# Gated linear attention: projections two tiles ahead, states as 64-row matmuls, f32r parts

## The reference

```python
q1 = (x @ Wq).reshape(B, L, H, DK) * scale          # H = 8 heads of DK = 64
k1 = (x @ Wk).reshape(B, L, H, DK)
v  = (x @ Wv).reshape(B, L, H, DV)
q2 = (x @ Wqa @ Wqb).reshape(B, L, H, DK) * scale   # low rank, 64
k2 = softmax((x @ Wka @ Wkb).reshape(B, L, H, DK))
gk1 = log_sigmoid(x @ Wg1a @ Wg1b + bg1) / 16       # low rank, 16
gk2 = log_sigmoid(x @ Wg2a @ Wg2b + bg2) / 16
e = softmax(x @ We); mask = one_hot(top_1(e)); rw = e * mask      # 4 experts
o = gla(q1, k1, v, gk1) + sum over experts of gla(q2 * rw, k2 * rw, v, gk2 * mask)
g = x @ Wga @ Wgb
o = rms_norm(o) * norm_w * (g * sigmoid(g))
return o @ Wo
```

## Time and profile before

| | us |
|---|---|
| median of 3 runs (lowest, highest) | 5345.69 (5344.24, 5350.46) |
| span of the profiled execution | 5273.1 |
| outside the span (median less span) | 72.6 |
| low_rank | 4213.0 to 4320.5 |
| linear_attention | 4320.5 to 5273.1 |
| TensorE busy, whole span | 4750.9 (90%) |
| VectorE busy, whole span | 4145.9 (79%) |
| ScalarE busy, whole span | 3061.5 (58%) |
| GpSimd busy, whole span | 1117.5 (21%) |

### The profile page before, as it was taken

The page is one execution under the profiler, slowest core; times in us unless marked ns, Lnnn a source line. Parts: engine busy times, 40 slices in busy tenths (PEclk is TensorE's granted clock), DMA queues, the critical chain, the costliest instruction groups (busy, mean ns, idle before and its releaser), DMA issues. The chain is left out here.

```text
span 5273.1 us, 101047 instructions
## 1 busy us (share of the span) xinstructions
PE 4750.9 (90%) x39176; PEld 2433.6 (46%) x39176; DVE 4145.9 (79%) x5059; ACT 3061.5 (58%) x5260; POOL 1117.5 (21%) x1152
## 2 busy tenths in 40 slices
PE   5579999999999999999999988558999969999998
PEld 3223333333333333333333356435666646666666
DVE  4489999999999999999999233377765447877877
ACT  1138888888888888888888712112222225555554
POOL 0000011202112021121211220254420004344443
PEclk8669999999999999999999999879999979999999
DMA  5434422322222222222221127632210030110100
...
DMA packets 236953, 421.64 MB, mean 80 GB/s; under 512 B 36745, under 2 KB 141210, under 8 KB 236432
## 3 DMA queue, kind: packets, MB, share of 16 engines
...
## 5 line engine op out<-in xcount | busy, mean ns | idle before, releaser
L956 DVE TENSOR_REDUCE attn_mpart<-attn_ps_max 128x2 f32<-128x1024 f32 x2048 | 2474.7, 1223 | 94.8 <-PE attn_ps_max L1007 85.1
L821 ACT ACTIVATE attn_probs<-attn_ps_exp 128x512 f32<-128x512 f32 x4096 | 2230.6, 595 | 411.0 <-PE attn_ps_exp L1023 331.3
L1007 PE MATMUL attn_ps_max<-attn_keys,attn_quer 54*128 54x512 f32 x4096 | 1474.0, 461 | 104.5 <-DVE attn_mpart L956 62.4
L1023 PE MATMUL attn_ps_exp<-attn_quer,attn_keys 54*128 54x512 f32 x4096 | 1513.3, 448 | 21.8 <-DMA attn_quer<-m_rows 20.7
L1038 PE MATMUL attn_ps_out<-attn_probs,attn_vals 128*32 128x256 f32 x16384 | 1312.1, 392 | 9.8 <-ACT route_o L826 9.2
L1023 PEld LDWEIGHTS attn_ps_exp<-attn_quer,attn_keys 54*128 54x128 f32 x4096 | 620.0, 185 | 860.1 <-ACT attn_probs L821 769.3
L1038 PEld LDWEIGHTS attn_ps_out<-attn_probs,attn_vals 128*32 128x32 f32 x16384 | 323.6, 108 | 750.8 <-issue 416.4
L1007 PEld LDWEIGHTS attn_ps_max<-attn_keys,attn_quer 54*128 54x128 f32 x4096 | 589.5, 189 | 169.7 <-DVE attn_mpart L956 106.0
L577 POOL DMA_INDIRECT x_rows<-route_pay,route_now x256 | 252.3, 985 | 431.7 <-DMA x_rows<-route_pay,route_now 359.5
L1576 POOL DMA_INDIRECT ra_rows<-y_rows,slots x256 | 255.5, 998 | 316.2 <-DVE ra_total L1743 244.5
L1707 ACT ACTIVATE ra_row<-ra_psS 128x512 f32<-128x512 f32 x112 | 66.9, 597 | 369.9 <-PE ra_psS L1628 369.9
...
## 6 DMA issues: line engine op xcount, KB each, us to landing
attn_keys<-k_laid SPq DMA_DIRECT2D x256, 304.0 KB
attn_vals<-v_aug SPq DMA_DIRECT2D x128, 512.0 KB, 16.1
attn_keys<-k_laid SPq DMA_DIRECT2D x256, 128.0 KB
...
```

Of the source, the lines that this page charges most:

```text
L821: act.activation(probs[k % 2][:, j, :], ps_exp[bank_of(g, n)][:, :], ACT.Exp).then_inc(exp_done, 1)
L956: dve.tensor_reduce(mpart[i][:, kb, TC * pair + tile::TC * NPR], ps_max[buffer][:, :, :], AX, ALU.max).then_inc(unit_read, 1)
L1007: mm = pe.matmul(ps_max[buffer][:, h, :], quer[at % NG][half(h), pair, tile * P:(tile + 1) * P], keys[at % 2][half(h), pair, kb * CH:(kb + ...
L1023: pe.matmul(ps_exp[bank_of(g, n)][:, :], keys[g % 2][half(h), pair, k * P:(k + 1) * P], quer[g][half(h), pair, :], start=True, stop=True). ...
```

## The change

What it does, by parts:

- **Four tiles in an iteration**: far, nxt, cur, prv. Z1, Z2 and ZG are made for far, between and behind the two halves of inter(cur); the rest of nxt's items in the next iteration. run has one more iteration to fill.
- **Order of TensorE**: turn_feats, scores 0, K2 Q2, decay_sums, keys_values, V, scores 1, turn_o, intra, G1 G2, project_o, K1 Q1, inter of two pairs, Z1 Z2 of far, inter of the others, ZG of far. ScalarE: decays(cur) ahead of abs and exp of nxt. VectorE: states are aged with the next tile's mean square; decay_states and log_sigmoid stand ahead of the second mask.
- **f32r parts**: every projection is made of f32r matmuls. Operands are split into a high part (a copy) and the rest (a subtraction): V, K1, Q1 are 6 matmuls each instead of 2 (high x high, high x low, low x high, for 2 blocks of rows), G1, G2 two each, ZG, K2, Q2 two each (both parts stacked in 128 rows), Z1, Z2 one each (three parts in 48 rows). In all 30 f32r matmuls of 512 columns per tile. The splits are new work: weights in low_rank (ScalarE 128x3072, 128x4096 and 128x128, GpSimd the rests), low in low_rank (ScalarE and GpSimd, 128x1024 per chunk), hT in linear_attention (hch on ScalarE, hcl on GpSimd, 128x256 per tile) and the log sigmoids (lsh on ScalarE, lsl on VectorE, 128x1024 per tile).
- **States without zero blocks**: s_mid is 128x1280 for a tile instead of 128x2560; inter is 40 matmuls of 64 rows and 64 columns, odd heads in one PSUM bank and even ones in another. decay_states, the addition and the ageing are one operation each over 128 partitions, and the addition is cut in two (dense, experts). pdec shares a bank of psO, so decay_sums waits until the former sums have been read (o_read), and intra waits for dec.
- **Space and DMAs**: xres's space holds ke and the states, so rope_attention stores xres to DRAM (x_mid, 8 stores of 512 KB) and linear_attention loads a tile of it for the output, which is one addition now (gb is multiplied into wo). low_rank stores 12 pieces of low per chunk instead of one. Linear_attention's weights load in low_rank. A tile has 7 loads instead of 4, and that of x_mid.

The diff, cut to its core:

```diff
+        def store_rows(sp, c):
+            sp.wait_ge(step, added(c * TC + TC - 1))
+            tiles = slice(c * TC, (c + 1) * TC)
+            sp.dma_start(x_mid[:, tiles, :], xres[:, tiles, :]).then_inc(x_stored, 16)
...
-                        hold(sp, low_copied, 2 * (c + 1), sp_passed)
-                        sp.dma_start(low_d[:, :, bass.ds(c * CH, CH)], low[i][:, :, :]).then_inc(low_stored[i], 16)
+                        hold(sp, low_parts, c + 1, sp_passed)
+                        n = bass.ds(c * CH, CH)
+                        high, rest = lowh[i], lowl[i]
+                        for g, r in ((0, LOW_G1[1]), (1, LOW_G2[1])):
+                            for x, part in enumerate((high, rest, high)):
+                                sp.dma_start(lz_d[g, x * GLR:(x + 1) * GLR, n],
+                                             part[r:r + GLR, 1, :].bitcast(F32)).then_inc(low_stored[i], 16)
+                        for x, (b, r) in enumerate((LOW_GATE, LOW_K, LOW_Q)):
...
+                act.wait_ge(g_loaded, 112)
+                act.wait_ge(tri_step, 5)
+                act.activation(gw.qkv[0][:, :, :, :], qkv[:, :, :, :], ACT.Copy).then_inc(w_high, 1)
+                act.activation(gw.up[:, :, :], up[:, :, :], ACT.Copy).then_inc(w_high, 1)
...
+        def run(eng, first, iteration, epilogue):
+
+            first((0, 0, 0))
+            iteration((1, 0, 1), (0, 0, 0), None, None)
+            iteration((2, 1, 0), (1, 0, 1), (0, 0, 0), None)
+            iteration((3, 1, 1), (2, 1, 0), (1, 0, 1), (0, 0, 0))
...
+                def iteration(far, nxt, cur, prv):
+                    if prv is not None:
+                        square(prv)
+                    if cur is not None:
+                        copy_feats(cur)
                     if nxt is not None:
-                        log_sigmoids(nxt, cur)
-                    else:
+                        copy_gate(nxt)
+                    if cur is not None:
                         decays(cur)
                     if nxt is not None:
+                        log_sigmoids(nxt)
```

```diff
-                def iteration(nxt, cur, prv):
+                def iteration(far, nxt, cur, prv):
                     if prv is not None:
                         mean_square(prv)
-                    if nxt is not None:
-                        add_bias(nxt)
-                        center(nxt)
-                    mask_scores(cur, 0)
-                    if prv is not None:
+                        age(prv)
                         scale_o(prv)
                         gated(prv)
-                    mask_scores(cur, 1)
+                    if cur is not None:
+                        mask_scores(cur, 0)
+                    if nxt is not None:
+                        center(nxt)
+                    if cur is not None:
+                        decay_states(cur)
                     if nxt is not None:
                         log_sigmoid(nxt)
-                    decay_states(cur)
-                    add_to_states(cur)
+                    if cur is not None:
+                        mask_scores(cur, 1)
+                        add_dense(cur)
+                    if nxt is not None:
+                        split_ls(nxt)
+                    if cur is not None:
+                        add_experts(cur)
```

```diff
-                        mm = pe.matmul(ps, (cen[:, :], m2c[i][:, 1, :])[x], ls[i][:, x, :], start=True, stop=True)
+                        pe.wait_ge(ls_low, m + 1)
+                        for part in (lsh, lsl):
+                            mm = pe.matmul(ps, (cen[:, :], m2g[i][:, :])[x], part[:, x, :], start=(part is lsh),
+                                           stop=(part is lsl))
...
+                                mm = pe.matmul(ps, h_part[:, k, :], w_part[:, x, k, :], start=(k == 0 and w_part is wqkv[0]
+                                               and h_part is hch), stop=(k == KD - 1 and h_part is hcl))
+                    elif item in (Z1, Z2):
+                        mm = pe.matmul(ps, lcz[i][:, :], wup[:, (UP_Z1, UP_Z2)[item - Z1], :], start=True, stop=True)
...
-                        (b, r), rows = {Z1: (LOW_G1, GLR), Z2: (LOW_G2, GLR), ZG: (LOW_GATE, LORA), K2: (LOW_K, LORA),
-                                        Q2: (LOW_Q, LORA)}[item]
-                        mm = pe.matmul(ps, lc[i][r:r + rows, b, :], wup[r:r + rows, b, :], start=True, stop=True)
+                        x, blocks = {ZG: (0, (UP_GATE, UP_GATE_LOW)), K2: (1, (UP_K, UP_K_LOW)),
+                                     Q2: (2, (UP_Q, UP_Q_LOW))}[item]
+                        for n, block_ in enumerate(blocks):
+                            mm = pe.matmul(ps, lcg[i][:, x, :], wup[:, block_, :], start=(n == 0), stop=(n == 1))
...
+                    pe.wait_ge(o_read, m)
...
+                    pe.wait_ge(dec_exped, m + 1)
+                    for odd in (1, 0):
+                        if odd == 0:
+                            pe.wait_ge(dense_read, m + 1)
...
+                def inter(tile, pairs):
                     m, _, i = tile
                     pe.wait_ge(state_set, m + 1)
                     pe.wait_ge(qe_ready, m + 1)
-                    for b in range(NPAIR):
-                        o = psO[:, 2 * b:2 * b + 2, :].rearrange("p h d -> p (h d)")
+                    for b in pairs:
                         for e in range(NS):
-                            queries = qeT[:, b, e - 1, :] if e else ftT[:, 1, b, :]
-                            mm = pe.matmul(o, queries, s_mid[:, b, e, :, :].rearrange("p h d -> p (h d)"),
-                                           start=False, stop=(b == NPAIR - 1 and e == NE), skip_group_check=True)
-                    mm.then_inc(intra_inter, 1)
-
-                def iteration(nxt, cur, prv):
+                            for odd in range(2):
+                                rows = slice(odd * DK, odd * DK + DK)
+                                queries = qeT[rows, b, e - 1, :] if e else ftT[rows, 1, b, :]
+                                mm = pe.matmul(heads_out[:, b, odd, :], queries, s_mid[rows, b, e, :], start=False,
+                                               stop=(b == NPAIR - 1 and e == NE), skip_group_check=True)
+                    if pairs[-1] == NPAIR - 1:
+                        mm.then_inc(intra_inter, 1)
...
+                def iteration(far, nxt, cur, prv):
                     ahead = lambda *items: [project(nxt, x) for x in items] if nxt is not None else None
-                    ahead(Z1, Z2)
-                    turn_feats(cur)
-                    ahead(ZG, K2)
-                    scores(cur, 0)
-                    decay_sums(cur)
-                    scores(cur, 1)
-                    ahead(Q2, V)
+                    if cur is not None:
+                        turn_feats(cur)
+                        scores(cur, 0)
+                    ahead(K2, Q2)
+                    if cur is not None:
+                        decay_sums(cur)
+                        keys_values(cur)
+                    ahead(V)
+                    if cur is not None:
+                        scores(cur, 1)
                     if prv is not None:
                         turn_o(prv, cur)
-                    keys_values(cur)
+                    if cur is not None:
+                        intra(cur)
+                    ahead(G1, G2)
                     if prv is not None:
                         project_o(prv, cur)
-                    ahead(G1, G2)
-                    intra(cur)
                     ahead(K1, Q1)
-                    inter(cur)
-
-                def prologue(tile):
-                    for x in range(NP):
+                    if cur is not None:
+                        inter(cur, (0, 1))
+                    if far is not None:
+                        project(far, Z1)
+                        project(far, Z2)
+                    if cur is not None:
+                        inter(cur, (2, 3))
+                    if far is not None:
+                        project(far, ZG)
+
+                def first(tile):
+                    for x in (Z1, Z2, ZG):
```

334 lines of the change are left out of this document (211 added, 123 removed).

## The result

| | median us (lowest to highest, runs) |
|---|---|
| before | 5344.97 (5335.64 to 5350.46, 4) |
| changed | 5499.26 (5458.79 to 5514.64, 4) |
| ratio | 1.0274, 95% interval 1.0226 to 1.0322 |

The changed kernel is slower by 154 us. The time lies 0.74 us inside the upper end of the range, which is luck: part of the 154 us isn't the change's, and the second comparison, which says 111, would have lain well inside. That later comparison of the same two kernels gave 5470.70 (5461.84 to 5497.61, 4 runs) against 5359.95, ratio 1.0229 (1.0180 to 1.0278).

A forecast was written before the change was run, and what follows sets the result against it. TensorE's own list bounds the kernel now; after the change a closed chain across engines would. Chain +37.5, clock dips +32 and edges +15 made +84.5 us on the median 5345.7: 5430, range 5310 to 5500.

The forecast's parts named there:

- The closed chain: linear_attention's loop: waits across TensorE, ScalarE and VectorE set a tile at 29.22 us against 27.97, +37.5 in 30.
- K1,Q1: Term of a tile's chain on TensorE: 12 f32r matmuls at 0.213 us each, 2.56 in all.
- The clock: linear_attention's tiles: 3 us idle brings dips in most, 1.5 us each, +32 net (bounds 0 and +84).
- The 64-row matmuls: Rival, inter: pairs pass in half the time, 4.56 to 2.28 us, total 5330 or 5294; chance 0.26.
- An f32r matmul at 0.33: Rival, projections: 24 f32r matmuls on the path cost 2.8 us more a tile, +84, total 5515; chance 0.14.
- a clock that holds: Rival, tile loop: the chain lengthens tiles but adds no dips, total 5398 (5380 to 5410); chance 0.20.
- The second chain: After inter: square, root, scale_o and gate could delay decay_sums; costed at nothing, with a microsecond to spare.
- x_mid's tail: End of rope_attention: the last 512 KB store of x_mid must land first, +3.7 us.
- Start of linear_attention: Weights no longer load there, so TensorE's first matmul comes at 7 us instead of 15.3: -8.
- SyncE's stores: low_rank: 13 stores issued per chunk instead of 2, 7.0 to 8.5 us a chunk, +5.5 (0 to +11).
- ScalarE's copies and GpSimd's subtractions: low_rank: weight copies ahead of the softmax's exp +6.9 us, subtractions beside the small softmax steps +3.
- the 72.6 us outside the span stay: Whole launch: median 5345.7 less profiled span 5273.1 was taken as fixed, so the +84.5 was added to the median.

The follow-up runs named there:

- y3: The changed kernel with the six matmuls of V issued three times over in each tile: 5353.44 us, ratio 1.0131 to the kernel before.
- x1: The kernel before with only x_mid's eight stores added in rope_attention, read by nobody: 5351.17 us against 5366.06, ratio 0.9989.

## Why the prediction was right, and where it was short

**The closed chain.** Right, term by term but one. From the tile above, measured against forecast: first feature turn to scores 3.19 (3.17); scores 1.09 (1.09); K2,Q2 1.13 (1.05); decay_sums to dec's end 1.36 (1.35); abs to the log sigmoid 5.83 (5.72); G1,G2 1.03 (1.05); from project_o to K1 2.19 (2.10); inter with Z1,Z2 5.41 (5.39); ZG 0.57 (0.63). Log sigmoid and masks to intra took 3.40 (3.03), with the turn of o already at the lower clock. The one term that was clearly too small is K1,Q1, 3.00 instead of 2.56: at full clock an f32r matmul of 512 columns follows the one before after 0.233 us, not after the 0.213 that I had worked out from the clock and not from a row, and the first of the twelve and the change of shape cost 0.1 each on top. At full clock the chain is 29.98 us (y3), forecast 29.22.

**The clock.** Right in kind: a dip in every tile, in the turn of o and intra, behind the wait. I took 1.5 us for each, and it is 31.62 - 29.98 = 1.64. That this came so near is luck: half of a full dip was a guess between bounds of 0 and 3.24. Of the signs, the tiles of 31.1 to 32.6 us lie above the 29 to 31 that I named, and low_rank's 22 above the 10 to 20. Over 30 tiles the loop is 948 us, forecast 922: 23 us of the difference is the chain's 0.76, 4 the clock.

**Rivals.** The 64-row matmuls don't pass in half the time: inter is two pieces of 2.37 and 2.38 us, each with a change of shape, for what took 4.56 before. The price of pairs was rightly read from the scores; that the loading of the weights sets it, as I wrote, no run here tests. An f32r matmul at 0.33 and a clock that holds are refuted too. The second chain, by way of scale_o, was never last: on VectorE the normalised output is done at 4917.8, and decay_sums starts at 4918.24. Its cover was 0.5 us and not the microsecond that I gave it; the ageing of the states now stands beside GpSimd's first small step and makes that 1.07 us longer (last section).

**The edges.** x_mid's tail 3.6 us (3.7). Start of linear_attention 6 us earlier (8): the first matmul comes at +9.3. SyncE has issued the seven loads 4.4 us into the stage, and the last one has landed only 4.9 us later; the 2.5 us that I put there had no row. Filling: the first inter comes 62.0 us into the stage (62.3 before), so the new stage costs what the start gains, 6 (4). low_rank +22.0 (15.4): the mis-sized term is SyncE's stores, +16.7 instead of +5.5. From the first store of hT to the last lie 69.1 us instead of 52.4: 9 of it is the last six chunks at 8.6 us, just above my upper bound of 8.5, and 7.7 is the gap behind the first chunk (result), which I had not thought of. Behind the last store the stage is 5.4 us longer, where I had 9.9 for ScalarE's copies and GpSimd's subtractions. One term was missing: in the last full iteration, which has no far and no nxt, nothing hides the waits for the copies, and it takes 23.2 us instead of 19.3.

**The sum against the stages.** The change's own stages are about 125 us longer, forecast 84.5. The 40 us between are the chain's 23 and the clock's 4, low_rank's 7, the last iteration's 4 and the 4 at the start and in the filling. So the steps were right and the sizes of the f32r matmul and of low_rank's stores too small.

**The premise that was wrong** is the one that set the sum on the median: "the 72.6 us outside the span stay". There is no such time. In every launch that had both, the time is the span and 1.6 us. By its span (5273.1) and its rope_attention (821.0) the profiled execution of the kernel before ran on a chip of the faster kind and the timed ones on a slower; the difference then sits in attention and rope_attention, whose instructions are the same. It did no harm here, since only differences within one trace were used, but a share of the whole reckoned from it would have been wrong. And it made the first comparison of traces point at rope_attention, which took x1 to refute.

**What remained.** 154 us measured in the first comparison, 111 in the second (medians), about 125 by the stages that the change touches. I can't account for the 43 us between the first two. The two profiled executions of the changed kernel differ by 24.7 us (5484.9 and 5460.2), and all of that lies ahead of rope_attention, in stages with the same instructions; what the other launches did is not on record.
